# A pre-norm decoder layer on one core: the attention's outputs in the second half by seven block products for eight

## The reference

```python
probs = jax.nn.softmax(scores, axis=-1)
out_lat = jnp.einsum('bhst,btr->bhsr', probs, c_kv)
wuv = w_uv.reshape(H, DV, KVL)
out = jnp.einsum('bhsr,hdr->bhsd', out_lat, wuv)
out = out.transpose(0, 2, 1, 3).reshape(b, s, H * DV)
return out @ w_out
```

## Time and profile before

| | before |
|---|---|
| median of 3 runs | 2042.65 us |
| the profiled execution's span | 2041.3 us |
| PE, DVE, ACT, POOL busy | 2036.0, 1190.8, 778.8, 491.0 us |
| granted TensorE clock | 1.000 |
| moved by DMA | 294.52 MB, 144 GB/s on average |

### The profile page before, as it was taken

The page is one execution under the profiler, slowest core; times in us unless marked ns, Lnnn a source line. Parts: engine busy times, 40 slices in busy tenths (PEclk is TensorE's granted clock), DMA queues, the critical chain, the costliest instruction groups (busy, mean ns, idle before and its releaser), DMA issues.

```text
span 2041.3 us, 29819 instructions
## 1 busy us (share of the span) xinstructions
PE 2036.0 (100%) x10640; PEld 1722.9 (84%) x10640; DVE 1190.8 (58%) x1977; ACT 778.8 (38%) x2031; POOL 491.0 (24%) x453
## 2 busy tenths in 40 slices
PE   9999999999999999999999999999999999999999
PEld 7788888888888888888888888888888778888887
DVE  6766666666666666665666666666567772332322
ACT  5443535344444444333333333333333455232221
POOL 5442424233333333211221222122221311000000
PEclk9999999999999999999999999999999999999999
DMA  9846445353535353585424435242344481202011
GB/s 361 331 138 225 141 146 182 104 190 100 185 107 179 107 199 114 209 300 176 150 66 149 133 99 174 72 154 81 130 139 186 146 308 42 83 0 83 1 42 42
DMA packets 69219, 294.52 MB, mean 144 GB/s; under 512 B 7329, under 2 KB 8097, under 8 KB 59553
## 3 DMA queue, kind: packets, MB, share of 16 engines
q1 hardware_dynamic: 69152, 293.64, 42.1%
HBM read 182.99 MB, written 110.62 MB: 144 GB/s over the span
## 4 chain that ended last, share of the span: by engine, by line
PE 99%; DVE 0%; DMA 0%; ACT 0%; issue 0%; DVEq 0%; ACTq 0%; SPq 0%
PE at_out L53 12%; PE at_out L55 12%; PE at_out L54 11%; PE at_qbank L55 7%; PE at_qbank L53 7%; PE at_qbank L54 7%; PE at_qbank L1168 6%; PE at_qbank L1169 6%; PE at_score L944 6%; PE at_score L942 3%; PE at_turned L950 3%; PE at_value L55 2%; PE at_value L54 2%; PE at_value L53 2%; PE at_value L1185 1%; PE at_value L1186 1%
## 5 line engine op out<-in xcount | busy, mean ns | idle before, releaser
L1912 DVE TENSOR_TENSOR at_acc<-at_out,at_acc 128x512 f32<-128x512 f32 x512 | 352.2, 688 | 116.3 <-PE at_out L55 109.9
L53 PE MATMUL at_out<-at_wvo,at_val_hi 128*128 128x512 f32 x1024 | 414.1, 404 | 0.0
L55 PE MATMUL at_out<-at_wvo,at_val_lo 128*128 128x512 f32 x1024 | 401.4, 392 | 0.0
L54 PE MATMUL at_out<-at_wvo,at_val_hi 128*128 128x512 f32 x1024 | 400.1, 391 | 0.0
L1325 ACT ACTIVATE at_probs<-at_probs,at_row_stats 128x128 f32<-128x128 f32 x512 | 199.8, 391 | 353.7 <-DVE at_row_stats L1890 353.7
L1603 POOL TENSOR_TENSOR at_probs<-at_probs,at_row_stats 128x512 f32<-128x512 f32 x128 | 133.1, 1040 | 586.0 <-DVE at_row_stats L1895 586.0
L55 PEld LDWEIGHTS at_out<-at_wvo,at_val_lo 128*128 128x128 f32 x1024 | 192.2, 188 | 44.3
L54 PEld LDWEIGHTS at_out<-at_wvo,at_val_hi 128*128 128x128 f32 x1024 | 193.3, 189 | 33.8
L53 PEld LDWEIGHTS at_out<-at_wvo,at_val_hi 128*128 128x128 f32 x1024 | 193.1, 189 | 33.9 <-DVE at_acc L1912 0.5
L1331 ACT ACTIVATE at_pT_hi<-at_turned 128x512 fp32r<-128x512 f32 x128 | 76.3, 596 | 317.1 <-PE at_turned L950 317.1
L1903 DVE TENSOR_TENSOR at_val_lo<-at_value,at_val_hi 128x512 fp32r<-128x512 f32 x128 | 88.5, 691 | 179.1 <-ACT at_val_hi L1335 179.1
(11 more groups left out here) (236 smaller groups left out, 4134.7 us busy)
## 6 DMA issues: line engine op xcount, KB each, us to landing
wvo_d<-at_wvo SPq DMA_DIRECT2D x16, 2048.0 KB, 10.4
parts_d<-at_rope_parts SPq DMA_DIRECT2D x32, 1024.0 KB, 7.1
at_qrope<-parts_d SPq DMA_DIRECT2D x128, 256.0 KB, 5.4
at_wvo<-wvo_d SPq DMA_DIRECT2D x16, 2048.0 KB, 8.4
ab_raw<-in_w_heads SPq DMA_DIRECT2D x32, 576.0 KB, 6.1
cr_ctx<-in_context SPq DMA_DIRECT2D x32, 512.0 KB, 6.6
wabs_d<-at_wabs SPq DMA_DIRECT2D x16, 768.0 KB, 8.0
at_wabs<-wabs_d SPq DMA_DIRECT2D x16, 768.0 KB, 5.4
```

The lines of the kernel that those rows point to most:

```text
L53: pe.matmul(out, w_hi, x_hi, start=first, stop=False)
L54: pe.matmul(out, w_hi, x_lo, start=False, stop=False)
L55: return pe.matmul(out, w_lo, x_hi, start=False, stop=last)
L1912: dve.tensor_tensor(at, outb[n][:], at, ALU.add).then_inc(added, 1)
```

## The change

The step's output is a product of 2x2 blocks: the values of two sequences by two heads (A11, A12; A21, A22) times the two heads' matrices by two column halves (b11, b12; b21, b22). In the second group these eight block products become seven, each in three passes, after the scheme of Winograd:

- The weights get four combinations t1 to t4 (t3 = b22 - b12 and so on). They are made once, in the first group, when a head is taken: whole by DVE (`take_head`), high by ACT (`make_high`), low by POOL (`make_low`). Seven blocks a pair, 3584 KB, are stored and reloaded instead of 2048 KB. The first group goes on with eight products.
- The values get four sums S1 to S4 a step. ACT copies the values whole out of PSUM, DVE makes the sums in place in SBUF (three operations: 128, 128 and 256 columns), ACT the high parts in two copies, DVE the low part of the direct blocks (384 columns), POOL that of the sums (512 columns).
- P1 and P2 are copied out by ACT (`keep`) and added to `acc` by POOL, P6, P7, P5, P3 and P4 are added by DVE, five additions for four. P6, P5 and P3 run on in bank 0 on top of P1, and P4 in bank 1 on top of P7, so that each must wait until the state of the bank before it has been read.
- P7, which starts bank 1 anew, stands ahead of P5.
- PE's step begins with the scores; the transposes stand behind P1, the latent block between P6 and P7, the values between P5 and P3.
- In the last quad half a batch's moments for the cross attention stand between the additions of P7 and P5 (steps 1, 2, 3, 5, 6).
- The rotary parts are made in place in `rope_tmp`, several buffers and loads move, and some semaphores are shared.

The diff, cut to its core:

```diff
+    PRODUCTS, PLAIN = 7, 3
+    A11, A12, A22, A21 = (slice(j * SEQ, (j + 1) * SEQ) for j in range(4))
+    S3, S2, S4, S1 = (slice(j * SEQ, (j + 1) * SEQ) for j in range(PLAIN, PRODUCTS))
+    DIRECT, SUMS = slice(0, PLAIN * SEQ), slice(PLAIN * SEQ, PRODUCTS * SEQ)
...
+    FACTORS = {"P1": (A11, "b11", 0), "P2": (A12, "b21", 1), "P6": (S2, "t2", 0), "P5": (S1, "t1", 0),
+               "P7": (S3, "t3", 1), "P3": (S4, "b22", 0), "P4": (A22, "t4", 1)}
...
+        def order(m, s):
+            return ["P1", "P2", "P6", "P7", "P5", "P3", "P4"]
...
+            def product(m, s, name, start=False):
+                pair, _ = place(s)
+                val, op, n = FACTORS[name]
+                out, hi, lo, weight = outb[n][:], val_hi[s % 2][:, val], val_lo[s % 2][:, val], wvo[pair][op]
+                pe.matmul(out, hi, weight[:, 0], start=start, stop=False, skip_group_check=True)
+                pe.matmul(out, hi, weight[:, 1], start=False, stop=False, skip_group_check=True)
+                if name == "P1":
+                    pe.wait_ge(val_lo_done, STEPS * m + s + 1)
+                pe.matmul(out, lo, weight[:, 0], start=False, stop=True, skip_group_check=True).then_inc(out_ready, 1)
...
+                pe.wait_ge(val_hi_done, STEPS * m + s + 1)
+                pe.wait_ge(added, out_free(m, s, "P3"))
+                product(m, s, "P1", start=True)
...
+            def product_2(m, s):
+                pe.wait_ge(added, out_free(m, s, "P4"))
+                product(m, s, "P2", start=True)
+            def product_6(m, s):
+                pe.wait_ge(val_sums_lo, later(m, s) + 1)
+                pe.wait_ge(staged, STAGED * later(m, s) + 1)
+                product(m, s, "P6")
...
+            def product_5(m, s):
+                pe.wait_ge(added, adds_later(m, s) + 1)
+                product(m, s, "P5")
+            def product_3(m, s):
+                pe.wait_ge(added, adds_later(m, s) + 1 + before_product(m, s, "P5"))
+                product(m, s, "P3")
+            def product_4(m, s):
+                pe.wait_ge(added, adds_later(m, s) + 1 + before_product(m, s, "P7"))
+                product(m, s, "P4")
...
+            def slot_second(m, s, end, kind, first):
+                next_scores(m, s, end, kind, first)
+                product_1(m, s)
+                if s + 1 < end:
+                    turn(m, s + 1)
+                product_2(m, s)
+                product_6(m, s)
+                next_latent(m, s, end, kind, first)
+                if order(m, s)[3] == "P7":
+                    product_7(m, s)
+                    product_5(m, s)
+                else:
+                    product_5(m, s)
+                    product_7(m, s)
+                if s + 1 < end:
+                    values(m, s + 1, group_of(kind, s + 1))
+                else:
+                    cross_turn(1)
+                product_3(m, s)
+                product_4(m, s)
+                if s in ROPE_AT and end > STEPS:
+                    next_rope(m, s, kind, first)
...
+            def make_high(q, p):
+                for op in MADE:
+                    act.wait_ge(made, first_made(q, p) + MADE.index(op) + 1)
+                    act.activation(high_of(p, op), made_whole[p][op], ACT.Copy).then_inc(made_hi, 1)
+            def keep(m, s, name):
+                z = ("P1", "P2").index(name)
+                act.wait_ge(pool_added, pool_adds_later(m, s) - STAGED + z + 1)
+                act.wait_ge(out_ready, outs_later(m, s) + z + 1)
+                act.activation(stage[z][:], outb[FACTORS[name][2]][:], ACT.Copy).then_inc(staged, 1)
...
+            def direct_values(m, s):
+                act.wait_ge(value_ready, STEPS * m + s + 1)
+                act.activation(val_whole[s % 2][:, 0:CH], value[:], ACT.Copy).then_inc(val_in, 1)
+                act.wait_ge(val_in, later(m, s) + 1)
+                act.activation(val_hi[s % 2][:, DIRECT], val_whole[s % 2][:, DIRECT], ACT.Copy).then_inc(val_hi_done, 1)
+            def value_sums(m, s):
+                act.wait_ge(val_sums, 3 * later(m, s) + 3)
+                act.activation(val_hi[s % 2][:, SUMS], val_whole[s % 2][:, SUMS], ACT.Copy).then_inc(val_sums_hi, 1)
...
+            def value_sums(m, s):
+                pool.wait_ge(val_sums_hi, later(m, s) + 1)
+                pool.tensor_tensor(val_lo[s % 2][:, SUMS], val_whole[s % 2][:, SUMS], as_f32(val_hi[s % 2][:, SUMS]),
+                                   ALU.subtract).then_inc(val_sums_lo, 1)
+            def add(m, s, z):
...
+                pool.wait_ge(staged, STAGED * later(m, s) + z + 1)
+                if z:
+                    pool.wait_ge(pool_added, pool_adds_later(m, s) + z)
+                pool.tensor_tensor(at, stage[z][:], at, ALU.add).then_inc(pool_added, 1)
...
+            def slot_second(m, s, end, kind, first):
+                finish = s - 1 in ROPE_AT and end > STEPS
+                add(m, s, 0)
+                if finish:
+                    rope_sums(first + USE[kind][s - 1] + 3)
+                add(m, s, 1)
+                if finish:
+                    rope_low(m + 1, ROPE_AT[s - 1])
+                if s + 2 < end:
+                    normalise(m, s + 2)
+                if s + 1 < end:
+                    value_sums(m, s + 1)
...
-            def take_head(h, use, part):
-                for n in range(2):
-                    cols = slice(h % 2 * D + n * CH, h % 2 * D + (n + 1) * CH)
+            def take_head(q, h, use, part):
+                whole, count = made_whole[h // 2], first_made(q, h // 2)
+                left, right = qbank[use % 2][:], qbank[(use + 1) % 2][:]
+                for n, of in ((0, left), (1, right)):
+                    weight = wvo[h // 2][block_of(h % 2, n)]
                     dve.wait_ge(ab_hi, part + n + 1)
-                    dve.tensor_tensor(wvo[h // 2][:, 1, cols], qbank[(use + n) % 2][:], as_f32(wvo[h // 2][:, 0, cols]),
-                                      ALU.subtract).then_inc(q_taken, 1)
+                    dve.tensor_tensor(weight[:, 1], of, as_f32(weight[:, 0]), ALU.subtract)
+                if h % 2 == 0:
+                    dve.tensor_tensor(whole["t1"], whole["t3"], left, ALU.subtract).then_inc(made, 1)
+                    dve.wait_ge(made, count + 1)
+                else:
+                    dve.tensor_tensor(whole["t2"], right, whole["t1"], ALU.subtract).then_inc(made, 1)
+                    dve.tensor_tensor(whole["t3"], right, whole["t3"], ALU.subtract).then_inc(made, 1)
+                    dve.wait_ge(made, count + 2)
+                    if not (isinstance(q, int) and (q, h) == (0, 1)):
+                        dve.wait_ge(t4_out, 16 * 2 * (2 * q + h // 2))
+                    dve.tensor_tensor(whole["t4"], left, whole["t2"], ALU.subtract).then_inc(made, 1)
+                    dve.wait_ge(made, count + 4)
+                dve.sem_inc(q_taken, 2)
...
+            def value_sums(m, s):
+                done, of = 3 * later(m, s), val_whole[s % 2]
+                dve.wait_ge(val_in, later(m, s) + 1)
+                dve.tensor_tensor(of[:, S1], of[:, A22], of[:, A21], ALU.add).then_inc(val_sums, 1)
+                dve.wait_ge(val_sums, done + 1)
+                dve.tensor_tensor(of[:, S2], of[:, S1], of[:, A11], ALU.subtract).then_inc(val_sums, 1)
+                dve.wait_ge(val_sums, done + 2)
+                both = of[:, S3_TO_S4].rearrange("p (j t) -> p j t", t=SEQ)[:, 0:3:2]
+                dve.tensor_tensor(both, of[:, A11_A12].rearrange("p (j t) -> p j t", t=SEQ),
+                                  of[:, S3_S2].rearrange("p (j t) -> p j t", t=SEQ), ALU.subtract).then_inc(val_sums, 1)
+            def direct_values(m, s):
+                dve.wait_ge(val_hi_done, STEPS * m + s + 1)
+                dve.wait_ge(val_sums, 3 * later(m, s) + 3)
+                dve.tensor_tensor(val_lo[s % 2][:, DIRECT], val_whole[s % 2][:, DIRECT],
+                                  as_f32(val_hi[s % 2][:, DIRECT]), ALU.subtract).then_inc(val_lo_done, 1)
+            def add_product(m, s, name, bl, n):
...
+                dve.wait_ge(out_ready, outs_later(m, s) + order(m, s).index(name) + 1)
+                if name == order(m, s)[4]:
+                    dve.wait_ge(added, adds_later(m, s) + 2)
+                dve.tensor_tensor(at, outb[FACTORS[name][2]][:], at, ALU.add).then_inc(added, 1)
...
+            def slot_second(m, s, end, kind, first):
+                use = USE[kind]
+                if s + 2 < end:
+                    largest(m, s + 2)
+                if s + 1 < end:
+                    turn(m, s + 1)
+                add_product(m, s, "P6", 1, 0)
+                late = order(m, s)[3] == "P7"
+                beside = NORMS_IN_LAST.get(s) if kind == "last" else None
+                if late:
+                    add_product(m, s, "P7", 1, 1)
+                if beside is not None:
+                    cross_half_moments(beside, 0)
+                if s // 2 + 2 < end // 2:
```

(59 more changed lines are left out.)

397 lines of the change are left out of this document (247 added, 150 removed).

## The result

The changed kernel takes 2062.3 us (median of 4 runs, 2062.03 to 2062.72) against 2042.52 (4 runs, 2042.22 to 2043.1) for the one before on the same chip: ratio 1.0097, 95% interval 1.0083 to 1.0111. It is slower by about 19.8 us; the forecast was 2062.5.

What follows compares the result with a forecast made beforehand. PE's instruction stream was taken as the bound: -43.8 + 21.3 + 3 + 23.8 + 11.6 + 2 + 2 = +19.9 us, on the median 2062.5 us. Its own range was 2047 to 2079; 8 in 10, 2022 to 2085.

Steps and rivals of the forecast that it cites:

- PE's stream: 64 steps of the second group: 24 output matmuls become 21, 192 go at 0.228 each, -43.8 us; plain step 9.39.
- P3's wait: P3 waits for DVE to add P5's result from bank 0: +0.38 a step in 56 steps, +21.3 us.
- P1's third pass: Plain steps: next P1's third pass wants DVE's 384-column subtraction, up to 0.1 late; 0.07 in 42 steps, +3 us.
- Behind a rotary block: Twice a quad DVE's sums wait for POOL at the shared SBUF ports; P1 starts 1.70 late in 14 steps, +23.8 us.
- Last quad and cross attention: Last quad +11.6 us from moments between additions and missing cover for waits; cross attention +1, sixth x1 tile asked for late.
- First half: Making t1 to t4 per pair of heads delays step 7 behind an odd head: 0.3 left, times 7, +2 us.
- the bound that the prediction set itself: Sign of being wrong: the first half grows by over 5 us.
- Switch: At the switch two 3 MB stores go ahead of the reloads of rotary weights and queries: +1 us.
- Reloads: Second half: rotary weights behind 3584 KB land after 13 us, PE wants them at 19; no cost.
- The rivals: No exclusion 0.20 (2038.5), waits covered 0.12 (2014), POOL first in every step 0.11 (2101), reloads become the wait 0.05 (2081).
- no exclusion: Short DVE sums slip in beside POOL; second and third sum behind a rotary block take 0.3; 2038.5 us, chance 0.20.
- P3's line: Sign: PE's waits list P3 behind a DVE addition, 0.3 to 0.4 us in nearly every step; missing means wrong.

Runs made afterwards that it cites:

- p5_psum: Changed kernel with P5 ahead of P7 again in quads 8 to 14 and one operand of each value sum in the values' PSUM bank: 2022.34 us.

## Why the prediction was right, and where it was not

- *PE's stream, -43.8.* Right: a plain step without waits takes 9.39, in p5_psum, for the forecast's 9.39.
- *P3's wait, +21.3.* Right in place and kind; 0.44 for 0.38, the rest being the 0.11 before the second pass, so 24.6. What the prediction doesn't say is that taking it away alone gives back 3.4: P1's chain was full to within 0.1 us.
- *P1's third pass, +3.* Wrong size, zero. The weight load waits 0.16 in 41 steps, but there was that much room; the matmul isn't late, and a plain step takes 9.82, the 9.39 and P3's 0.44.
- *Behind a rotary block, +23.8.* Right mechanism; such a step is 1.25 longer than before and a plain one 0.25 shorter, so 1.50 each instead of 1.70, 21.0 in 14. Counted from the step's first score (1301.40), POOL begins at 3.0 and ends its normalisation at 11.6, both as forecast; the third sum ends at 11.9 for 12.2, P3's addition at 12.5 for 12.8, P1 starts at 12.6 for 13.0, and without a wait it would start at 11.1 for 11.3.
- *Last quad and cross attention, +12.6.* Measured 5.7 + 5.5 = 11.2. Steps 1 to 3 are 0.8 to 0.9 longer than 9.39, for the forecast's 0.9; no experiment took this term apart.
- *First half, +2.* This step failed, by the bound that the prediction set itself (over 5 us). It counted only what DVE, ACT and POOL do more in a pair of heads. It had no line for the load into `rope_tmp`, which in the changed kernel must wait for the parts to be stored and stands behind their reloads in SyncE's queue, nor for t4's store. These made a stall of 5.3 us in one step, which the forecast had nowhere; some 1.6 of it, an estimate from the 3.2 us of matmuls at 0.50, is the lower clock. The step before it is 1.3 longer, the attention begins 0.6 earlier, and the other seven quads grow by 0.6 together, not by 0.3 each.
- *Switch, +1.* Zero; the 2 us in the starts of the transposes are their new place.
- *Reloads, nothing.* Right: no wait of PE on one in quads 8 to 14.

A quad takes 89.8 by SyncE's queue, within the forecast's 90 to 91 but for 0.2; the earlier trace rows gave 88.75:

```profile
1203.94 0.33 SPq L585 DMA_DIRECT2D at_wabs<-wabs_d  x1
...
1293.74 0.33 SPq L585 DMA_DIRECT2D at_wabs<-wabs_d  x1
```

That the time came out within 0.2 us is luck: an error of +4.6 (first half) stood against -1 (switch), -2.5 (quads 8 to 14) and -1.4 (last quad and cross attention), and the -2.5 are themselves +3.3, -3 and -2.8. What was not luck is the kind of the two large waits and the size of each within 0.2 us a step. The rivals are out: the second and third sum last 1.25 and 1.15 behind a rotary block, where "no exclusion" needed 0.3; P3's line is there; P6 waits for POOL's subtraction once, 0.5 us in the last step; no reload shows.
